# Signs of the second raw weights multiplied in by GpSimd in front of its additions instead of by ScalarE

## The reference, cut to what matters

```python
def spectral_conv(x, w1, w2):                    # x: b, 32 channels, 64, 64
    x_ft = jnp.fft.rfft2(x)
    out_ft[:, :, :M1, :M2]  = einsum('bixy,ioxy->boxy', x_ft[:, :, :M1, :M2],  w1)   # M1 = M2 = 12
    out_ft[:, :, -M1:, :M2] = einsum('bixy,ioxy->boxy', x_ft[:, :, -M1:, :M2], w2)
    return jnp.fft.irfft2(out_ft, s=(h, w))
...
for i in range(LAYERS):
    w1 = w1r[i] + 1j * w1i[i]
    w2 = w2r[i] + 1j * w2i[i]
    h = layer_norm(spectral_conv(h, w1, w2) + conv1x1(h, conv_w[i]) + conv_b[i])
    if i < LAYERS - 1: h = gelu(h)
```

## Time and profile before

| | |
|---|---|
| median of 3 runs | 5455.23 us (5449.39 to 5459.4) |
| time of the profiled execution | 5451.53 us |
| its span, first to last instruction | 5449.8 us |
| mean granted TensorE clock | 0.969 |
| busy, TensorE | 4984.3 us |
| busy, VectorE | 3838.4 us |
| busy, ScalarE | 3866.9 us |
| busy, GpSimd | 891.3 us |

### The profile page before, as it was taken

One profiled execution on the slowest core, in us unless ns is written; L12 is line 12 of the kernel. 1 busy time (PEld: TensorE's weight loads), 2 busy tenths in 40 slices (PEclk: granted clock), 3 DMA queues, 4 the chain that ended last, 5 costly groups with the idle time before them and its releaser, 6 DMA issues.

```text
span 5449.8 us, 134904 instructions
## 1 busy us (share of the span) xinstructions
PE 4984.3 (91%) x43556; PEld 2874.9 (53%) x43556; DVE 3838.4 (70%) x7702; ACT 3866.9 (71%) x6261; POOL 891.3 (16%) x1359
## 2 busy tenths in 40 slices
PE   5888899999999999999999999999999999768777
PEld 2444567666767666776667734433333333334433
DVE  4888899888989888998888955555455554354454
ACT  5999877888767888777887766677777777523333
POOL 0134221333212332222332200000000000000000
PEclk9999999999999999999999999999999999878888
DMA  1344567677777676776677722311111111000000
GB/s 63 136 144 165 158 204 242 230 236 231 241 236 238 225 241 226 250 247 229 224 241 238 243 82 69 70 47 55 48 51 54 47 54 47 11 4 4 8 8 4
DMA packets 222595, 756.33 MB, mean 139 GB/s; under 512 B 74033, under 2 KB 113202, under 8 KB 156730
## 3 DMA queue, kind: packets, MB, share of 16 engines
q1 hardware_dynamic: 175162, 632.45, 33.9%
q0 software_dynamic: 47104, 119.60, 8.9%
HBM read 397.49 MB, written 354.42 MB: 138 GB/s over the span
## 4 chain that ended last, share of the span: by engine, by line
PE 59%; DVE 13%; ACT 12%; issue 11%; DMA 2%; SPq 1%; ACTq 1%; DVEq 1%; POOL 0%; POOLq 0%
PE ps_y L924 9%; PE ps_t L1030 8%; PE ps_t L936 5%; PE ps_y L916 5%; PE ps_f L924 4%; PE ps_f L1015 4%; PE ps_t L945 4%; ACT big L1174 3%; PE ps_t L1039 2%; PE ps_s L961 2%; ACT big L1183 2%; PE ps_y L1000 2%; DVE big L1358 2%; DVE big L1339 2%; ACT big L1178 2%
## 5 line engine op out<-in xcount | busy, mean ns | idle before, releaser
L1358 DVE TENSOR_REDUCE big<-big 128x16 f32<-128x512 f32 x1280 | 857.0, 680 | 677.2 <-ACT big L1174 674.4
L1351 DVE TENSOR_TENSOR big<-big 128x512 f32<-128x512 f32 x1280 | 886.7, 699 | 32.9 <-DVE big L1380 18.6
L1174 ACT ACTIVATE big<-ps_y 128x512 f32<-128x512 f32 x892 | 550.2, 617 | 470.1 <-PE ps_y L924 417.6
L1190 ACT ACTIVATE big<-ps_t,g_now 128x512 f32<-128x512 f32 x1024 | 823.5, 804 | 7.9 <-PE ps_t L936 7.9
L936 PE MATMUL ps_t<-ident,big 128*128 128x128 f32 x5120 | 793.1, 278 | 30.3 <-DVE big L1351 22.4
L924 PEld LDWEIGHTS ps_y<-conv_now,big 128*128 128x128 f32 x5088 | 617.2, 191 | 362.8 <-issue 362.8
L1183 ACT ACTIVATE big<-ps_t 128x512 f32<-128x512 f32 x1024 | 635.3, 620 | 158.5 <-PE ps_s L961 111.4
L924 PE MATMUL ps_y<-conv_now,big 128*128 128x128 f32 x5088 | 717.9, 284 | 0.0
L936 PEld LDWEIGHTS ps_t<-ident,big 128*128 128x128 f32 x5120 | 572.2, 141 | 275.5 <-issue 233.8
L945 PE MATMUL ps_t<-ident,big 128*128 128x128 f32 x4096 | 634.8, 278 | 70.3 <-ACT big L1183 65.0
L945 PEld LDWEIGHTS ps_t<-ident,big 128*128 128x128 f32 x4096 | 466.0, 142 | 227.5 <-issue 117.1
(11 more groups left out here) (197 smaller groups left out, 7619.5 us busy)
## 6 DMA issues: line engine op xcount, KB each, us to landing
hstore<-big SPq DMA_DIRECT2D x256, 1024.0 KB, 4.2
big<-hstore SPq DMA_DIRECT2D x256, 1024.0 KB, 5.3
xmodes<-x_out SPq DMA_DIRECT2D x128, 312.0 KB, 4.4
y_kt<-ymodes SPq DMA_DIRECT2D x512, 78.0 KB
ymodes<-y_st POOLq DMA_DIRECT2D x192, 144.0 KB, 5.7
ymodes<-y_st POOLq DMA_DIRECT2D x64, 192.0 KB, 5.4
mix_room<-xmodes POOLq DMA_DIRECT2D x32, 336.0 KB, 7.3
mix_room<-xmodes POOLq DMA_DIRECT2D x64, 168.0 KB, 9.0
```

The source lines that it names most:

```text
L1174: af(y_sq[wh], of[:, wh, :], ACT.Square).then_inc(s["sq_done"], 1)
L1190: af(h_new[k // 2][:, at:at + 512], ps_t1[:, :], ACT.Identity if kind == "stem" else ACT.Gelu, bias=g_now[:, 1:2], scale=g_now[:, 0:1]).th ...
L1351: v_.tensor_tensor(groups(y_sb[2 * k + wh]), groups(y_sb[2 * k + wh]), rstd[:, k // 2, at:at + 16].unsqueeze(2).to_broadcast([128, 16, 32] ...
L1358: v_.tensor_reduce(ss[:, k // 2, at:at + 16], groups(y_sq[wh]), AX.X, ALU.add).then_inc(s["ss_done"], 1)
```

## The change: what it does

ScalarE's `sign_w2` is gone. `sign_w1` now counts `w_scaled`. GpSimd multiplies `w2_raw` in place with a TENSOR_SCALAR of its own, in front of each addition and behind the same wait on `xhat_done`. In front of the first it waits for the raw weights too, in front of the second for its own first addition. Behind the multiplication it waits for it through a new semaphore, `w_signed`. `w_scaled` is still waited for, since the addition lands on what `sign_w1` wrote.

```diff
@@ add_weights, GpSimd
                 o0, done = rnd * OCH % CH, l * ROUNDS + rnd
                 then(pool, "xhat_done", 8 * n + 2 + 2 * second)
+                if second:
+                    then(pool, "w_added", 2 * done + 1)
+                else:
+                    then(pool, "w_raw", 128 * done + 128)
+                nc.gpsimd.tensor_scalar(w2_raw[:, :, :], w2_raw[:, :, :], c_sign[:, 4 + slot:5 + slot], None, ALU.mult
+                                        ).then_inc(s["w_signed"], 1)
+                then(pool, "w_signed", 2 * done + 1 + second)
                 then(pool, "w_scaled", 2 * done + 1 + second)
                 view, rev = weight_views(slot, slice(o0, o0 + OCH))
                 nc.gpsimd.tensor_tensor(view, view, rev, ALU.add).then_inc(s["w_added"], 1)
@@ sign_w1 and sign_w2, ScalarE
                 af(wslot[:, 0:M * M, slot, o].rearrange("p m o -> p o m"), w1_raw[:, :, :], ACT.Copy,
-                   scale=c_sign[:, slot:slot + 1])
-
-            def sign_w2(l, rnd, slot, second):
-                if second:
-                    wait(act, "w_added", 2 * (l * ROUNDS + rnd) + 1)
-                af(w2_raw[:, :, :], w2_raw[:, :, :], ACT.Copy, scale=c_sign[:, 4 + slot:5 + slot]).then_inc(s["w_scaled"], 1)
+                   scale=c_sign[:, slot:slot + 1]).then_inc(s["w_scaled"], 1)
@@ body, ScalarE, layer phases (the stem's branch loses the same two calls)
-                        if slots is not None and k == 3:
-                            sign_w2(ph, q - 8, slots[1], 1)
                         square(unit, 0, of)
...
                         if slots is not None and k == 1:
                             sign_w1(ph, q - 8, o, slots[0])
-                            sign_w2(ph, q - 8, slots[0], 0)
```

More of the change, by code:

```diff
@@ L126, in vit_tower @@
             "px_done", "f_done", "tw_done", "fw_done", "fw_read", "xout_done", "iw_done", "iw_read",
-            "x_low", "x_high", "first_low", "first_high", "mix_done", "mix_sum", "mix_read", "w_raw", "w_zero", "w_scaled", "w_added",
+            "x_low", "x_high", "first_low", "first_high", "mix_done", "mix_sum", "mix_read", "w_raw", "w_zero", "w_scaled", "w_signed", "w_added",
             "xt_done", "fc1_done", "g1_done", "fc2_done", "g2_done", "fc3_done", "tok_done", "tok_stored0", "tok_stored1")}
@@ L1283, in body @@
                             gelu(turned + wh, m, kt, wh, kind)
-                        if slots is not None and k == 3 and wh == 0 and front in STORED:
-                            sign_w2(ph, q - 8, slots[1], 1)
                         if front is not None:
```

## The result

The changed kernel's median is 5518.73 us (5515.03 to 5520.62, four runs), against 5452.57 us (5449.39 to 5459.4, four runs) for the kernel before in the same comparison: ratio 1.0122, interval 1.0107 to 1.0137. It is 66 us slower, where the prediction's number was 33 us slower. The profiled execution took 5515.03 us, with a span of 5513.3 us and a mean granted clock of 0.963.

What follows compares the result with a forecast made beforehand. It took one loop through ScalarE's k = 2 and 3 and VectorE's Newton chain to bound the kernel. Net losses of 18 (phases 1, 2), 14 (phase 3) and 1 us (stem) made 33, so 5455 + 33 = 5488 us; range 5445 to 5530.

Steps and rivals of the forecast that it cites:

- What bounds the kernel: In weight-work quads, one loop through ScalarE's k = 2 and 3 and the Newton chain's start; sign_w2 on it, 0.66 us.
- The relief, 52 us: ScalarE without sign_w2: 0.66 us less in 48 layer quads, 1.26 us less in 16 stem quads, if nothing else moved.
- T: Time of one added GpSimd TENSOR_SCALAR of 128 x 576, taken as 0.83 us from a copy's row.
- The bounds of T: GpSimd's multiplication between 0.53 us (memset) and 1.85 us (addition): 17 to 51 us, or 128 us, slower.
- Rival 3: GpSimd's multiplication costs what its addition costs: 60 to 128 us slower, 5515 to 5583 us; chance 0.10.
- The gaps: GpSimd's wait on its own semaphore behind the multiplication: 0.29 us with plain numbers, 0.6 us with a register (phases 1, 2).
- The multiplication as a partner: Cited rule: VectorE's two-SBUF-input instructions and GpSimd instructions reading SBUF exclude each other for the whole instruction.
- The Newton chain's TENSOR_SCALARs are held: On VectorE they stand behind GpSimd's second addition; in phases 1 and 2 the start comes 0.55 us later, 18 us.
- rival 1: ScalarE's relief wins since no addition holds the Newton chain's TENSOR_SCALARs: faster, 13 us at T = 0.53; chance 0.14.
- The three parts: Added time by quads: phases 1 and 2 0.55 us (18 us), phase 3 0.9 (14 us), stem 0.06 (1 us).
- the cover: Stem: L936 ends 0.81 us later, but gelu starts 0.75 us after its end anyway, leaving 0.06 us a quad.
- What was to be hidden: Next round's weight DMAs start 0.6 to 1.5 us later; in the stem 2.6 us of room before sign_w1 hides it.

Runs made afterwards that it cites:

- e1: The changed kernel with GpSimd's multiplications of w2_raw left out and the additions kept in place: 5405.76 us, ratio 0.9915 to the kernel before.
- e4: The changed kernel with GpSimd copying w2_raw onto itself instead of multiplying, signs left out: 5484.11 us, ratio 1.006 to the kernel before.
- e6: The changed kernel with only the second multiplication moved, right behind the first addition without the xhat_done wait: 5505.31 us, ratio 1.0094 to the kernel before.
- e3: The kernel before, ScalarE's sign_w2 kept, with GpSimd also multiplying an idle buffer of the same size in the same two places: 5534.35 us, ratio 1.0155.
- e5: The changed kernel with only half of the values multiplied (128 x 288), the rest keeping their sign: 5489.23 us, ratio 1.0072 to the kernel before.
- e2: The changed kernel with the first multiplication moved before order_x, the second right behind the first addition without the xhat_done wait: 5418.05 us, ratio 0.9938 to before.
- e8: e2 with the stem's second multiplication written to its own buffer and put in front of order_x: 5417.35 us, ratio 0.9935 to the kernel before.

## Why the prediction was right, and where its size was off

The direction, the mechanism and the range held; the number was short by half of the loss, and most of what it was short of is a term for the stem that it had at nothing.

**What bounds the kernel: right.** `sign_w2` was on the chain with 0.66 us a layer quad, and taking it away alone gives 0.65 to 0.67 (e1). The page's busy share of 91% on TensorE would have said nothing of either effect.

**The relief, 52 us: 45.5 measured.** The layers are as put; in the stem 2 x 0.63 = 1.26 us a quad were counted and 0.82 came. Twelve of e1's 15 stem steps are 20.85 us (1.13 less). The other three are 22.38 us, and they are the three that have 3.4 us at the lower clock.

**"The new instruction reads one tensor and writes one, like the copy: I take T = 0.83": a step that was off.** T is 1.72 us. The stand-in was itself close as a price of a copy (0.83 worked out, 0.67 measured); it is the likeness that fails. With the copy in its place the kernel loses 33 us (e4), with the TENSOR_SCALAR 66. That e4 lands on the prediction's 33 doesn't make T the whole of the miss: 17 of its 33 us are the stem's, for which the sum had 1. The bounds of T were wide enough to hold the truth, 0.53 and 1.85, and the row at the upper end was the near one. Rival 3 had T almost right and put 60 to 128 us on it: the measured 66 lies at its lower end. Its parts were 2.3, 1.55 and 1.9 us a quad for phases 1 and 2, phase 3 and the stem; 0.93, 0.39 and 1.89 came. The first two were too high for the two reasons that follow. The third is right by luck, as it had no term for the clock.

**The gaps: too long.** 0.6 us with a register and 0.29 with plain numbers were taken from the wait in front of a DMA issue. Behind the multiplication the trace shows 0.21 and 0.09 us.

**The multiplication as a partner: not for its whole length.** The bound for T = 1.85 comes out only if the multiplication holds `normed` to its end, as the addition does. In the changed kernel `normed` starts 1.0 us or more behind the multiplication's start and passes free, 64 times of 64. The rule of the Trainium skill cited in the prediction (SBUF — State Buffer, "Who interferes with whom") has the two exclude each other for the whole instruction. The trace of e6 agrees with it for the first 0.6 us of a multiplication and not behind that, and the measurement decides. That the next L1351 stands beside the addition, as the sum had it, is right.

**The Newton chain's TENSOR_SCALARs are held: right**, by an assumption that no row of before could bear out. L1360 took 1.77 us beside an addition and 0.52 us beside a multiplication. This is what undid rival 1, and e3 shows the consequence: ScalarE's relief ends in that hold and is worth nothing in the layers.

**The three parts** were 0.55, 0.9 and 0.06 us a quad (18, 14 and 1 us), and came out at 0.93, 0.39 and 1.89 (30, 6 and 30 us). Phases 1 and 2 follow from T. Phase 3 had the addition ready just ahead of `normed`; with the longer T `normed` comes first, and the late part is the second addition alone. In the stem the lateness itself was well put: from the end of the pair of `normed` to the Newton chain's second two-input instruction it is 7.22 us before (321.58 to 328.80) and 8.23 us after (329.93 to 338.16), 1.0 us against the 0.81 worked out. What failed first is the cover, the 0.75 us by which ScalarE came late in front of one `gelu`. The prediction followed the lateness to that `gelu` alone, but TensorE's own next work starts late with it, and the chain now runs from the held Newton chain over L943, L897, L952, L943 and L981 on TensorE. With this the step is 0.77 us longer in the quads that keep their clock. What failed second has no term in the prediction at all: TensorE's granted clock, 1.00 in every stem quad before, is 0.50 for 6.8 us in nine of 15 steps after, and this is the other 1.12 us.

**What was to be hidden was hidden.** The weight DMAs start later, and no `sign_w1` waits for them anywhere in the trace (ScalarE has no idle time in front of L1215). The quad's steps, the short `normed` followed by a long one, and the addition's end on L1360's hold are what the last paragraph of the prediction asked for; "nothing in the stem", the 104 us of ScalarE (67 measured) and the 0.66 us by which VectorE's wait in k = 3 was to shrink (1.44 to 0.97 us in the quads shown) are not.

## What to carry to other kernels

Before work is moved to an engine that is 16% busy, look at what its instructions lock: here 1.72 us of idle GpSimd time cost more than 0.66 us of busy ScalarE time, because it made an addition late that stops VectorE on the critical loop. Move the work in front of the wait that it doesn't need, not behind it: with the same two multiplications the kernel is 66 us slower behind the waits and 33 us faster ahead of them, and only both moves together do it, since each late one is enough by itself. Look at the granted clock by quads, not only by its mean: 0.969 before and 0.963 after look alike, and about 18 of the 66 us lie between them. And compare the parts of a sum with the steps, not only its total: e4 and e5 came out near their numbers with parts that were wrong. A stand-in for the price of an unseen instruction wants a second look when another row of the same engine, of the same size, is twice as far: an instruction with a scalar per partition was priced like an addition and not like a copy.

## What the runs showed of the hardware that was not expected

- GpSimd's TENSOR_SCALAR with a scalar per partition takes 1.72 us for 128 x 576 fp32 values and 1.00 us for 128 x 288, so 2.5 ns a value and 0.28 us apart from it. A copy of 128 x 576 takes 0.67 us, the addition 1.85.
- GpSimd's TENSOR_SCALAR (1.72 us) doesn't hold VectorE for its whole length. A TENSOR_TENSOR of 128 x 512 that starts 0.09 to 0.51 us behind it ends 1.28 to 1.31 us behind its start (e2, e6), and one that starts 0.6 us behind it or later takes 0.64 to 0.69 us (372 times). A TENSOR_SCALAR of 128 x 64 is held if it starts before 0.6 us or from 1.07 us on, then to the end, and free between (0.2 us, 15 times). Beside GpSimd's addition the TENSOR_TENSOR of 128 x 512 takes up to 1.48 us and the TENSOR_SCALAR up to 1.79 us (after). Beside GpSimd's copies two TENSOR_TENSORs take 1.67 us in place of 1.25 (e8). A multiplication that starts while a held `normed` is still finishing takes 1.96 us (e2, e6). Why the hold has these two parts wasn't tested.
- TensorE's granted clock fell from 1.00 to 0.50 in the stem for 3.4 or 6.8 us at a time, beside idle times of 1.89 to 2.60 us in front of L943; L897's four matmuls took 2.08 us in place of 1.13 there. It fell in e1 as well (3.4 us in three of 15 steps), where TensorE is never idle for more than 0.79 us, and it stayed in four steps of the changed kernel with idle times of 2.04 to 2.25 us. So the longest idle time alone doesn't tell.
- The engine that comes second pays: 2.28 us for an addition 0.10 us behind `normed`, 2.16 us for a `normed` 0.23 us behind an addition (e5).
